# A pairwise embedding product with an MLP on one core: embeddings turned through the U slots and copied by VectorE

## The chip, the cores and the metric

The kernel runs on 1 core of one Trainium2 chip. The metric is the device time of one execution in microseconds (us); lower is better. The kernel before takes 458.64 us, the median of 3 runs (458.62 to 458.97).

The engines are called by the names that the profile uses: PE is TensorE's matmul stream and PEld its weight loads, DVE is VectorE, ACT is ScalarE, POOL is GpSimd and SP is SyncE, which here only issues DMAs.

## The reference

For each of 1024 rows of the batch, 32 embeddings e_0 ... e_31 of 64 numbers are fetched from 32 tables by index. For each of the 496 pairs i < j there is a 64 x 64 matrix K_ij, and the pair's result is one number:

```python
e = stack([tbl_f[ids[:, f]] for f in range(32)], axis=1)      # [1024, 32, 64]
p, q = e[:, ROW_IDX], e[:, COL_IDX]                           # all pairs i < j, 496 of them
z = einsum('bne,hne,bnh->bn', p, kernel, q)                   # z[b, n] = q_n^T K_n p_n
h = concatenate([z, dense_ctx], axis=1)                       # [1024, 496 + 16]
h = maximum(h @ W_top1 + b_top1, 0)                           # 512
h = maximum(h @ W_top2 + b_top2, 0)                           # 256
y = h @ W_top3                                                # [1024, 1]
```

Everything is float32.

## The kernel before

**Tiles and blocks.** The batch is cut into 8 tiles of 128 rows. In a tile the pairs are worked through in 32 blocks (n = 0 to 31). A block has 16 places of 64 numbers: for a pair of fields 2m and 2m+1 (the two halves) it holds the products with up to 8 lower fields i. `plan_blocks` (L44) lays the blocks out in four groups of 2, 6, 10 and 14 blocks; group g needs fields up to 8g+7.

**One block.** PE computes U = K times the turned embedding of the upper field into a U slot, two PSUM banks of `u_ps`. There are three slots (`USLOTS`, L70), used in turn, so PE can be at most three fills ahead of DVE. `block_u` (L374) waits for the slot with `multiplied`, and for the turned embedding with `side_copied`. DVE (`multiply`, L314) multiplies the slot by the lower embedding into SBUF, which frees the slot. Blocks come in two kinds of 16 each. In a straight block the batch row is on the partitions, and the sums over 64 numbers are made by ACT (12 places at most, one activation with an accumulator read each, L264) and DVE (4 places, one reduce, L346), in the order of the blocks; products wait for ACT in a ring of 5 buffers. Straight blocks have one matmul per half ("whole", 8 of them) or two ("split", 8 of them, two DVE products). In a turned block the batch row is on the free axis, 16 matmul records fill the slot, and the sums are made by PE: `pick_sums` (L400) multiplies the product by a 0/1 matrix, 8 matmuls per block (16 records), into the bank `side_ps`.

**The side bank.** `side_ps` is one PSUM bank that all other PE work goes through, step by step: `bank_steps` (L142) writes the order of its uses down, and PE may start a step only when ACT has copied the one before (`side_free`, L360). Its uses in a tile are the four `turn_group` steps, which turn the next tile's embeddings (128x128 transposes against the identity, four per group, L370) and which ACT copies to `emb_t` (L255); the picks of the first eight turned blocks and of the last eight, each in two runs of four; and, for the tile before, `spread` (h0 turned, L421), `hidden1` (L425), `hidden2` (L430) and `logit` (L434). All engines work through their own list in order. The list of PE places these steps after fixed blocks (L136 to L139): 

```python
LATE_SUMS_AT = (0, 2)
MLP_AT = {5: "spread", 8: "hidden1", 11: "hidden2", 13: "logit"}
SUMS_AT = (20, 22)
TURN_AT = {24: 0, 26: 1, 28: 2, 30: 3}
```

In tile 0 each group is turned just before its first block. ACT copies a turned group in its own order, between its sums.

**Loads.** POOL gathers the embeddings with one indirect DMA per field, 32 per tile, in order of tile and field (L222), into three buffers; a fourth tile's gathers wait until the first is used up. PE waits for a group's eight gathers before it turns it. SP issues the indices of all tiles (128 KB), the identity, then all 16 K loads of 512 KB at once, with the pick matrix after the fourth; then the dense features, the weights and the biases. PE's first wait is for the identity and the pick matrix together.

## Time and profile before

| | |
|---|---|
| median of 3 runs | 458.64 us |
| the profiled execution's own time | 458.04 us |
| its span, first to last instruction | 456.2 us |
| mean granted TensorE clock | 0.985 |
| PE busy | 398.2 us (87%), 5424 matmul records |
| PEld busy | 303.2 us (66%) |
| DVE busy | 342.2 us (75%), 448 instructions |
| ACT busy | 337.5 us (74%), 2937 instructions |
| POOL busy | 241.9 us (53%) |

Busy time is the time in which the engine executes at least one instruction; matmuls are pipelined, so a busy PE isn't PE at its peak. A second look at the same execution is the map of its 40 slices of 11.4 us each (a digit is the busy share of the slice in tenths; for PEclk it is the granted clock in tenths; for DMA the busy share of the queues). It shows three stretches: a start of four or five slices with the DMA queues full and PE mostly idle, a long regular stretch, and a short end.

```
PE   0354959899989999899989999999989998999986
DVE  0036857797988798787888798778888798779880
ACT  1048554798778996798778986798769986898662
POOL 5777777777777777777777776377700000000000
PEclk9998879999999999999999999999999999999999
DMA  8991111111111111111111111011100000000000
```

The profiler lists, for the whole span, which engine sat idle and what ended each wait. A wait is a loss only where the waiting engine is the one that others wait for.

### The profile page before, as it was taken

Reading aid. Unit: us, or ns where it says so; the run is one execution under the profiler, and the core shown is the slowest. Engines: PE = TensorE matmul, PEld = TensorE weight load, DVE = VectorE, ACT = ScalarE, POOL = GpSimd, SP = SyncE. Lnnn points to the kernel's source line nnn. Section 1 sums busy time; section 2 is a strip of 40 time slices with the busy share of each in tenths; the row PEclk is TensorE's granted clock in tenths of the full one; section 3 lists DMA queues with packets and bytes.
Section 4 is the critical chain, followed back from the end, with each engine's and each line's share of the span. In section 5 each row is a group of like instructions: output and inputs, shape, how many; then the busy total and the mean of one; then the engine's idle time right before and its main releaser. Section 6 shows DMA issues by size and latency. Waiting matters only on the chain.

```text
span 456.2 us, 15136 instructions
## 1 busy us (share of the span) xinstructions
PE 398.2 (87%) x5424; PEld 303.2 (66%) x5424; DVE 342.2 (75%) x448; ACT 337.5 (74%) x2937; POOL 241.9 (53%) x260
## 2 busy tenths in 40 slices
PE   0354959899989999899989999999989998999986
PEld 0232647677767767677767867777767776777765
DVE  0036857797988798787888798778888798779880
ACT  1048554798778996798778986798769986898662
POOL 5777777777777777777777776377700000000000
PEclk9998879999999999999999999999999999999999
DMA  8991111111111111111111111011100000000000
GB/s 273 385 309 30 27 27 27 30 28 28 30 28 29 29 28 27 29 31 27 30 28 29 28 28 27 12 29 26 29 7 4 2 3 1 4 1 1 4 3 0
DMA packets 14553, 19.62 MB, mean 43 GB/s; under 512 B 7176, under 2 KB 7824, under 8 KB 14480
## 3 DMA queue, kind: packets, MB, share of 16 engines
q0 software_dynamic: 8192, 8.40, 9.9%
q1 hardware_dynamic: 6288, 10.27, 6.6%
q8 instruction: 43, 0.70, 0.7%
q14 instruction: 30, 0.25, 0.2%
HBM read 18.65 MB, written 0.00 MB: 41 GB/s over the span
## 4 chain that ended last, share of the span: by engine, by line
PE 52%; DVE 18%; ACT 13%; issue 11%; POOL 3%; DMA 2%; DVEq 0%
PE u_ps L387 15%; PE side_ps L409 12%; PE u_ps L394 12%; DVE prod_s L336 11%; ACT prod_s L264 10%; PE side_ps L425 7%; DVE h L346 4%; PE side_ps L430 3%; POOL emb L222 3%; DVE prod_t L323 3%; PE side_ps L370 2%; DMA emb<-tbl,ids_sb 1%; ACT emb_t L255 1%; DMA ids_sb<-ids 1%; ACT h_t L278 1%
## 5 line engine op out<-in xcount | busy, mean ns | idle before, releaser
L264 ACT ACTIVATE prod_s<-prod_s 128x64 f32<-128x64 f32 x1408 | 297.0, 324 | 62.4 <-DVE prod_s L336 61.6
L222 POOL DMA_INDIRECT emb<-tbl,ids_sb x256 | 241.7, 944 | 89.2 <-issue 77.4
L264 ACT ACTIVATION_READ_ACCUMULATOR prod_s<-prod_s 128x1 f32 x1408 | 276.0, 239 | 0.0
L336 DVE TENSOR_TENSOR prod_s<-u_ps,emb 128x384 f32<-128x384 f32 (+3 forms) x192 | 159.2, 860 | 53.3 <-PE u_ps L394 53.3
L323 DVE TENSOR_TENSOR prod_t<-u_ps,emb_t 128x1024 f32<-128x1024 f32 x128 | 155.9, 1218 | 46.9 <-PE u_ps L387 46.8
L387 PEld LDWEIGHTS u_ps<-emb_t,k_sb 64*128 64x128 f32 x2048 | 130.5, 192 | 54.2 <-issue 40.2
L387 PE MATMUL u_ps<-emb_t,k_sb 64*128 64x128 f32 x2048 | 144.7, 284 | 16.2 <-ACT emb_t L255 10.8
L394 PE MATMUL u_ps<-k_sb,emb_t 64*128 64x512 f32 (+4 forms) x768 | 141.8, 485 | 1.4 <-ACT emb_t L255 1.4
L394 PEld LDWEIGHTS u_ps<-k_sb,emb_t 64*128 64x128 f32 x768 | 61.5, 195 | 19.2 <-issue 14.6
L409 PEld LDWEIGHTS side_ps<-prod_t,pick_sb 128*32 128x32 f32 x2048 | 54.1, 110 | 13.9 <-issue 13.1
L409 PE MATMUL side_ps<-prod_t,pick_sb 128*32 128x128 f32 x2048 | 62.5, 274 | 0.0
L346 DVE TENSOR_REDUCE h<-prod_s 128x4 f32<-128x256 f32 x128 | 52.4, 410 | 0.3
L370 PE MATMUL side_ps<-id_sb,emb 128*128 128x128 f32 x128 | 21.7, 294 | 31.1 <-DMA emb<-tbl,ids_sb 23.0
L370 PEld LDWEIGHTS side_ps<-id_sb,emb 128*128 128x128 f32 x128 | 14.0, 146 | 41.9 <-issue 33.0
L255 ACT ACTIVATE emb_t<-side_ps 128x512 f32<-128x512 f32 x32 | 21.8, 682 | 25.3 <-PE side_ps L370 25.3
L425 PE MATMUL side_ps<-h_t,w_sb 128*128 128x128 f32 x256 | 30.7, 278 | 4.1 <-ACT h_t L278 4.1
L425 PEld LDWEIGHTS side_ps<-h_t,w_sb 128*128 128x128 f32 x256 | 29.2, 192 | 5.7 <-ACT h_t L278 5.7
L273 ACT ACTIVATE h_t<-side_ps 128x128 f32<-128x128 f32 x16 | 6.2, 389 | 19.9 <-PE side_ps L409 19.9
L430 PEld LDWEIGHTS side_ps<-h_t,w_sb 128*128 128x128 f32 x128 | 14.9, 191 | 6.7 <-issue 5.3
L430 PE MATMUL side_ps<-h_t,w_sb 128*128 128x128 f32 x128 | 16.4, 281 | 1.2 <-ACT h_t L281 1.2
L281 ACT ACTIVATE h_t<-side_ps,b_sb 128x128 f32<-128x128 f32 x32 | 11.0, 612 | 3.9 <-PE side_ps L425 3.9
L284 ACT ACTIVATE h_t<-side_ps,b_sb 128x128 f32<-128x128 f32 x16 | 5.0, 364 | 3.8 <-PE side_ps L430 3.8
(12 smaller groups left out, 23.6 us busy)
## 6 DMA issues: line engine op xcount, KB each, us to landing
k_sb<-k_pairs SPq DMA_DIRECT2D x16, 512.0 KB, 11.1
emb<-tbl,ids_sb POOLq DMA_INDIRECT x256, 2.4
w_sb<-w SPq DMA_DIRECT2D x1, 1024.0 KB
w_sb<-w SPq DMA_DIRECT2D x1, 512.0 KB
ids_sb<-ids SPq DMA_DIRECT2D x1, 128.0 KB, 2.6
h<-dense SPq DMA_DIRECT2D x8, 8.0 KB
out<-y_row SPq DMA_DIRECT2D x8, 0.5 KB
id_sb<-ident SPq DMA_DIRECT2D x1, 64.0 KB, 2.8
```

The source lines that it names most:

```text
L222: nc.gpsimd.indirect_dma_start(emb[t % EMBS][:, f * EMBED:(f + 1) * EMBED], None, tables[f], bass.IndirectOffsetOnAxis(ap=ids_sb[:, t, f:f ...
L255: nc.scalar.activation(emb_t[t % 2][:, g * GROUP_PAIRS:(g + 1) * GROUP_PAIRS], side_ps[:], ACT.Copy,).then_inc(side_copied, 1)
L264: last = nc.scalar.activation(slot, slot, ACT.Copy, accum_out=acc_ps[:, t % 2, column:column + 1])
L323: last = nc.vector.tensor_tensor(prod_t[at % TRING][:].rearrange("p (h x) -> p h x", h=HALVES), u, low.unsqueeze(1).to_broadcast([P, HALVE ...
L336: last = nc.vector.tensor_tensor(product[:, :, cols], u[:, :, cols], low.unsqueeze(1).to_broadcast([P, HALVES, w * EMBED]), ALU.mult)
L346: nc.vector.tensor_reduce(h0[t][:, column:column + ON_DVE], product[:, cols].rearrange("p (n e) -> p n e", e=EMBED), AX_X, ALU.add,).then_ ...
L370: last = nc.tensor.transpose(side_ps[:, d], emb[t % EMBS][:, 2 * m * EMBED:(2 * m + 2) * EMBED], id_sb[:])
L387: last = nc.tensor.matmul(u[:, half * BANK + d * P:half * BANK + (d + 1) * P], k_sb[rows, n * BANK + d * P:n * BANK + (d + 1) * P], emb_t[ ...
L394: last = nc.tensor.matmul(u[:, half * BANK + s * EMBED:half * BANK + (s + w) * EMBED], emb_t[t % 2][rows, m], k_sb[rows, n * BANK + s * EM ...
L409: last = nc.tensor.matmul(side_ps[quad:quad + QUAD, 0], pick_sb[:, 30 - 2 * place:62 - 2 * place], prod_t[at % TRING][:, d * P:(d + 1) * P ...
L425: last = nc.tensor.matmul(side_ps[:, m], w1_sb[:, c, m * P:(m + 1) * P], h0_t[:, c], start=(c == 0), stop=(c == 3))
L430: last = nc.tensor.matmul(side_ps[:, m], w2_sb[:, c, m * P:(m + 1) * P], h1_t[:, c], start=(c == 0), stop=(c == 3))
```

## The change

1. **Turning.** The embeddings are no longer turned through `side_ps` by 128x128 transposes and copied by ACT. Each pair of fields is turned by two transposes of 64 batch rows each, one into each bank of a U slot, and DVE copies the slot to `emb_t`. A turn is thus a use of the U slots like a block's; `slot_uses` writes the order down, and `slot_filled` and `slot_emptied` count fills and copies or products. From tile 1 on, a tile is turned in two parts of eight pairs (16 fields), after blocks 24 and 28 of the tile before. In tile 0 there are seven parts: four pairs, then six times two.
2. **Block order.** The kinds and the order of the blocks in groups 1 to 3 are changed so that blocks come in order of the parts they need. There are again 16 turned and 16 straight blocks (8 whole, 8 split); the places that ACT sums are the same in number. The ring of turned products has 11 buffers in place of 10.
3. **Picks.** The picks of eight turned blocks come in one run: the first eight after block 21, preceded by the logit of the tile before, which lies in the same bank beside them; the last eight after block 6 of the next tile, followed by the transposes of h0 into other columns of the same bank, and ACT copies both at once. hidden1 comes after block 10, hidden2 after block 14.
4. **Loads.** The indices of tile 0 (16 KB) are loaded first, the others after the identity. K loads 1 to 15 wait on SP for the gathers of a part of tile 0; the pick matrix comes after the last K load, with a semaphore of its own. In `w1_rows` the rows of W_top1 are put in the new order on the host.

The core of the diff:

```diff
-    order = ["SS", "STSTSS", "TSTSTSTSTS", "TSTTSTTSTTSTTS"]
+    order = ["SS", "TSSTSS", "TSTTSTSTSS", "TSTTSTSTTSTTTS"]
...
-        turned = [fulls.pop(0) for _ in range(order[a].count("T"))]
-        straight = [x, *fulls, y]
-        blocks += [(turned.pop(0), True) if kind == "T" else (straight.pop(0), False) for kind in order[a]]
+        blocks += zip([*fulls[:2 * a], x, *fulls[2 * a:], y], [kind == "T" for kind in order[a]], strict=True)
...
+FIRST_PARTS = [(0, 4), (4, 6), (6, 8), (8, 10), (10, 12), (12, 14), (14, 16)]
+PARTS = [(0, 8), (8, 16)]
+PART_OF = [next(p for p, (_, stop) in enumerate(FIRST_PARTS) if max(m for m, _, _, _ in b) < stop) for b in BLOCKS]
+FIRST = [PART_OF.index(p) for p in range(len(FIRST_PARTS))]
...
-TRING = 10
+TRING = 11
...
+K_WITH_PART = [4, 6, 8, 10, 12, 14, 16]
+TURN_AT = {24: 0, 28: 1}
...
+def slot_uses():
...
             if t == 0 and n in FIRST:
...
+                uses.append(("turn", 0, FIRST.index(n)))
+            uses.append(("u", t, n))
+            if t + 1 < TILES and n in TURN_AT:
+                uses.append(("turn", t + 1, TURN_AT[n]))
...
+SPREAD_AT, HIDDEN1_AT, HIDDEN2_AT, SUMS_AT = 6, 10, 14, 21
...
-            pool.wait_ge(ids_loaded, 16)
+            pool.wait_ge(first_ids_loaded, 16)
             for t in range(TILES):
+                if t == 1:
+                    pool.wait_ge(ids_loaded, 16)
...
-            sp.dma_start(ids_sb[:], ids.rearrange("(t p) f -> p t f", p=P)).then_inc(ids_loaded, 16)
+            by_tile = ids.rearrange("(t p) f -> p t f", p=P)
+            sp.dma_start(ids_sb[:, 0], by_tile[:, 0]).then_inc(first_ids_loaded, 16)
             sp.dma_start(id_sb[:], ident).then_inc(id_loaded, 16)
-            for c in range(NB // K_PER_LOAD):
-                cols = slice(c * K_PER_LOAD * BANK, (c + 1) * K_PER_LOAD * BANK)
-                sp.dma_start(k_sb[:, cols], k_pairs[:, cols]).then_inc(k_loaded[c], 16)
-                if c == 3:
-                    sp.dma_start(pick_sb[:], pick).then_inc(id_loaded, 16)
+            sp.dma_start(ids_sb[:, 1:], by_tile[:, 1:]).then_inc(ids_loaded, 16)
+            c = 0
+            for p, stop in enumerate(K_WITH_PART):
+                while c < stop:
+                    if c == 1 or (c > 1 and c == K_WITH_PART[p - 1]):
+                        first, last = FIRST_PARTS[p]
+                        sp.wait_ge(first_gathered[p], 16 * 2 * (last - first))
+                    cols = slice(c * K_PER_LOAD * BANK, (c + 1) * K_PER_LOAD * BANK)
+                    sp.dma_start(k_sb[:, cols], k_pairs[:, cols]).then_inc(k_loaded[c], 16)
+                    c += 1
+            sp.dma_start(pick_sb[:], pick).then_inc(pick_loaded, 16)
...
-            def copy_turned(t, g):
-                act.wait_ge(side_ready, READY[f"turn{g}", t])
-                if t >= 2:
-                    act.wait_ge(multiplied, (t - 1) * NB)
-                nc.scalar.activation(emb_t[t % 2][:, g * GROUP_PAIRS:(g + 1) * GROUP_PAIRS], side_ps[:], ACT.Copy,
-                                     ).then_inc(side_copied, 1)
...
+            def copy_first_sums(t):
+                act.wait_ge(picked, t * NT + CHUNK)
+                if t > 0:
+                    copy_logit(t - 1)
+                nc.scalar.activation(h0_t[:, 0], side_ps[:, 0], ACT.Copy).then_inc(side_copied, 1)
+            def copy_spread(t):
+                act.wait_ge(mlp_mm, 3 * t + 1)
+                nc.scalar.activation(h0_t[:, 1:], side_ps[:, :3], ACT.Copy).then_inc(side_copied, 1)
...
                     if not TURNED[n]:
                         sum_block(t, n)
+                    if t > 0 and n == 0:
+                        copy_acc(t - 1)
+                    if t > 0 and n == SPREAD_AT:
+                        copy_spread(t - 1)
+                    if t > 0 and n == HIDDEN1_AT:
+                        hidden1(t - 1)
+                    if t > 0 and n == HIDDEN2_AT:
+                        hidden2(t - 1)
+                    if n == SUMS_AT:
+                        copy_first_sums(t)
...
+            def copy_turned(t, part):
+                at = SLOT_USE["turn", t, part]
+                dve.wait_ge(slot_filled, at + 1)
+                first, last = FIRST_PARTS[part] if t == 0 else PARTS[part]
+                turned_half = u_ps[at % USLOTS][:].rearrange("p (h m b) -> p m h b", h=HALVES, b=P // 2)
+                nc.vector.tensor_copy(emb_t[t % 2][:, first:last, :].rearrange("p m (h b) -> p m h b", h=HALVES),
+                                      turned_half[:, :last - first]).then_inc(slot_emptied, 1)
...
                     multiply(t, n)
+                    if t + 1 < TILES and n in TURN_AT:
+                        copy_turned(t + 1, TURN_AT[n])
                     if n > 0 and not TURNED[n - 1]:
                         sum_block(t, n - 1)
...
-            def turn_group(t, g):
-                pe.wait_ge(gathered[t % EMBS][g], 16 * GROUP * (t // EMBS + 1))
-                side_free(f"turn{g}", t)
...
+            def slot_free(at):
+                if at >= USLOTS:
+                    pe.wait_ge(slot_emptied, at - USLOTS + 1)
+                return u_ps[at % USLOTS]
+            def turn_part(t, part):
+                if t == 0:
+                    first, last = FIRST_PARTS[part]
+                    pe.wait_ge(first_gathered[part], 16 * 2 * (last - first))
+                else:
+                    first, last = PARTS[part]
+                    fills = t // EMBS if t % EMBS == 0 else t // EMBS + 1
+                    pe.wait_ge(gathered[t % EMBS][part], 16 * 2 * (last - first) * fills)
+                u = slot_free(SLOT_USE["turn", t, part])
+                for m in range(first, last):
+                    for half in range(HALVES):
+                        rows = slice(half * P // 2, (half + 1) * P // 2)
+                        at = half * BANK + (m - first) * P // 2
+                        done = nc.tensor.transpose(u[:, at:at + P // 2],
+                                                   emb[t % EMBS][rows, 2 * m * EMBED:(2 * m + 2) * EMBED],
+                                                   id_sb[rows, rows])
+                done.then_inc(slot_filled, 1)
...
+            def spread(t):
+                pe.wait_ge(side_copied, STEPS * t + 1)
+                pick_sums(t, 1)
+                pe.wait_ge(summed_v, (t + 1) * NS)
+                pe.wait_ge(acc_copied, t + 1)
+                for c in range(S_CHUNKS):
+                    last = nc.tensor.transpose(side_ps[:, 1 + c], h0[t][:, c * P:(c + 1) * P], id_sb[:])
+                last.then_inc(mlp_mm, 1)
...
                 for n in range(NB):
                     if t == 0 and n in FIRST:
-                        turn_group(0, FIRST.index(n))
+                        turn_part(0, FIRST.index(n))
                     block_u(t, n)
...
+                    if t > 0 and n == SPREAD_AT:
+                        spread(t - 1)
+                    if t > 0 and n == HIDDEN1_AT:
+                        hidden1(t - 1)
+                    if t > 0 and n == HIDDEN2_AT:
+                        hidden2(t - 1)
+                    if n == SUMS_AT:
+                        if t > 0:
+                            logit(t - 1)
+                        else:
+                            pe.wait_ge(pick_loaded, 16)
+                        pick_sums(t, 0)
                     if t + 1 < TILES and n in TURN_AT:
-                        turn_group(t + 1, TURN_AT[n])
+                        turn_part(t + 1, TURN_AT[n])
```

## Rows read from the trace of the kernel before

**Rows 1.** Windows, one regular tile: length, PE, PEld, DVE, ACT, POOL, clock, DMA, GB/s

```profile
218.56:269.33 50.77, 48.49 (x680) 36.99 (x681) 42.74 (x57) 41.89 (x370) 38.58 (x41) 1.00 0.16 29
```

**Rows 2.** Waits in that tile: who for whom, us in total, times, longest

```profile
DVE prod_t L323 <- PE u_ps L387: 4.7, 5, 1.5
DVE prod_s L336 <- PE u_ps L394: 3.3, 2, 2.3
...
PE side_ps L370 <- ACT emb_t L255: 1.2, 1, 1.2
...
PE side_ps L425 <- ACT h_t L278: 0.5, 1, 0.5
```

**Rows 3.** PE in order of time, tile 0: start us, duration us, what

```profile
44.91 2.08 PE L387 MATMUL u_ps<-emb_t,k_sb 64*128 64x128 f32 x16 [5.88 <-ACT emb_t L255]
...
63.13 2.08 PE L387 MATMUL u_ps<-emb_t,k_sb 64*128 64x128 f32 x16 [4.94 <-ACT emb_t L255]
...
85.24 0.66 PE L370 MATMUL side_ps<-id_sb,emb 128*128 128x128 f32 x4
```

**Rows 4.** POOL in order of time, the 1st, 48th and 64th gather

```profile
3.61 1.08 POOL L222 DMA_INDIRECT emb<-tbl,ids_sb  x1 [3.17 <-DMA ids_sb<-ids]
...
62.43 0.94 POOL L222 DMA_INDIRECT emb<-tbl,ids_sb  x1 [0.30 <-issue]
...
82.40 0.94 POOL L222 DMA_INDIRECT emb<-tbl,ids_sb  x1 [0.30 <-issue]
```

**Rows 5.** Gathers between 60 and 90 us, from issue to landing

```profile
DMA to landing us min/median/max: 2.2/2.4/3.3
```

**Rows 6.** DVE in order of time; first and last are block 31

```profile
87.11 1.29 DVE L336 TENSOR_TENSOR prod_s<-u_ps,emb 128x128 f32<-128x128 f32 x2
...
231.65 1.21 DVE L323 TENSOR_TENSOR prod_t<-u_ps,emb_t 128x1024 f32<-128x1024 f32 x1
232.78 0.41 DVE L346 TENSOR_REDUCE h<-prod_s 128x4 f32<-128x256 f32 x1
...
243.35 1.29 DVE L336 TENSOR_TENSOR prod_s<-u_ps,emb 128x128 f32<-128x128 f32 x2 [0.98 <-PE u_ps L394]
244.55 0.41 DVE L346 TENSOR_REDUCE h<-prod_s 128x4 f32<-128x256 f32 x1
244.88 1.28 DVE L336 TENSOR_TENSOR prod_s<-u_ps,emb 128x384 f32<-128x384 f32 x2
...
441.05 1.28 DVE L336 TENSOR_TENSOR prod_s<-u_ps,emb 128x128 f32<-128x128 f32 x2
```

**Rows 7.** PE in order of time, the regular stretch

```profile
226.71 2.06 PE L387 MATMUL u_ps<-emb_t,k_sb 64*128 64x128 f32 x32
228.70 0.66 PE L370 MATMUL side_ps<-id_sb,emb 128*128 128x128 f32 x4
229.28 1.13 PE L394 MATMUL u_ps<-k_sb,emb_t 64*128 64x512 f32 x4
...
240.17 1.96 PE L409 MATMUL side_ps<-prod_t,pick_sb 128*32 128x128 f32 x64
242.05 2.11 PE L394 MATMUL u_ps<-k_sb,emb_t 64*128 64x64 f32 x16
...
252.83 3.84 PE L425 MATMUL side_ps<-h_t,w_sb 128*128 128x128 f32 x32 [0.52 <-ACT h_t L278]
...
259.41 2.05 PE L430 MATMUL side_ps<-h_t,w_sb 128*128 128x128 f32 x16
```

**Rows 8.** PE at the end of the last tile

```profile
439.87 3.70 PE L409 MATMUL side_ps<-prod_t,pick_sb 128*32 128x128 f32 x128
```

**Rows 9.** ACT in the chain that ended last, a whole block's sums

```profile
249.90 2.57 ACT prod_s L264 x24
```

**Rows 10.** The chain that ended last, its first DMA: start us, us

```profile
0.74 2.60 DMA ids_sb<-ids
```

**Rows 11.** Windows, the 2 us after tile 0's second wait for ACT (clock third last)

```profile
64.00:66.00 2.00, 2.00 (x18) 1.98 (x18) 0.74 (x1) 0.00 (x0) 1.56 (x2) 0.50 0.24 41
```

More of the change, by code:

```diff
@@ L113, in w1_rows @@
 def w1_rows():
[L114 to L118 removed]
+    rows = [None] * (T_CHUNKS * P)
     for n in range(NB):
@@ L124, in w1_rows @@
                     chunk, quad, place = sum_place((T_INDEX[n] * HALVES + half) * LOW + d // 2)
[L125 to L144 removed]
+                    rows[chunk * P + quad + 2 * place + d % 2] = pair_row(i0 + d, 2 * m + half)
+    straight = [n for n in range(NB) if not TURNED[n]]
+    rows += [pair_row(i, j) for n in straight for s, i, j in places(n) if s in act_slots(n)]
+    rows += [pair_row(i, j) for n in straight for s, i, j in places(n) if s not in act_slots(n)]
+    return rows + list(range(PAIRS, PAIRS + DENSE))
+K_PER_LOAD = 2
+K_WITH_PART = [4, 6, 8, 10, 12, 14, 16]
+TURN_AT = {24: 0, 28: 1}
+def slot_uses():
+    uses = []
     for t in range(TILES):
@@ L438, in _, with hidden1 @@
-            pe.wait_ge(id_loaded, 32)
+            def spread(t):
[6 more added lines that the diff above has]
+                last.then_inc(mlp_mm, 1)
+            def hidden1(t):
+                pe.wait_ge(side_copied, STEPS * t + 2)
+                for m in range(4):
+                    for c in range(4):
+                        last = nc.tensor.matmul(side_ps[:, m], w1_sb[:, c, m * P:(m + 1) * P], h0_t[:, c],
+                                                start=(c == 0), stop=(c == 3))
+                last.then_inc(mlp_mm, 1)
@@ new lines, in hidden2, with logit @@
+            def hidden2(t):
+                pe.wait_ge(side_copied, STEPS * t + 3)
+                for m in range(2):
+                    for c in range(4):
+                        last = nc.tensor.matmul(side_ps[:, m], w2_sb[:, c, m * P:(m + 1) * P], h1_t[:, c],
+                                                start=(c == 0), stop=(c == 3))
+                last.then_inc(mlp_mm, 1)
+            def logit(t):
+                pe.wait_ge(side_copied, STEPS * t + 4)
+                for c in range(2):
+                    last = nc.tensor.matmul(side_ps[0:1, 1], w3_sb[:, c:c + 1], h2_t[:, c],
+                                            start=(c == 0), stop=(c == 1))
+                last.then_inc(logit_mm, 1)
@@ L439, in _ @@
+            pe.wait_ge(id_loaded, 16)
             for t in range(TILES):
```

184 lines of the change are left out of this document (61 added, 123 removed).

## The prediction

> **What bounds the kernel now.** I read the map of slices first, for the stretches; then the windows and the waits of one tile of the regular stretch; then DVE and PE in order of time; and then the start, PE's waits beside POOL's clock of gathers.
>
> A regular tile takes 50.77 us, with PE busy 48.49, DVE 42.74 and ACT 41.89 [rows 1]. DVE waits 8.0 us per tile for PE (4.7 + 3.3); PE's waits for ACT are only 1.2 (a turned group's copy) and 0.5 (the copy of h0) [rows 2]. So PE sets the pace, and DVE runs dry while PE does side work, since only three slots lie between them.
>
> In tile 0 PE waits 5.88 and 4.94 us for ACT, whose copies of turned groups queue behind its sums; its last turn of tile 1's embeddings starts at 85.24 [rows 3]. That is close behind the 64th gather, issued at 82.40 [rows 4], which with the median landing of 2.4 us [rows 5] is there at 84.8. POOL needs 1.25 us per gather, 40 per tile: tile 0 to tile 1 is bound by POOL within half a microsecond, whatever PE and ACT do before.
>
> I lay the time out by one mark, the start of DVE's product of block 31. It is at 87.11 in tile 0 and 441.05 in tile 7 [rows 6], so the span of 456.2 is 87.1 (start), 6 x 50.77 = 304.6, 49.3 for tile 7, and 15.15 (end).
>
> **Prices.** DVE, from one start to the next: a turned product 1.13, a reduce 0.33, a split product 1.20, followed by its own reduce 1.33 (87.11 to 88.44 also is one, as block 31) [rows 6]. A whole product moves as many numbers as a turned one; I take 1.13 too. PE: a turned block 0.99, a split block 1.02, a whole one 0.86 to 0.97, four transposes with their switches of mode 0.58, 64 pick records 1.88, hidden1 3.8, hidden2 2.0 [rows 7]. 128 pick records in one run take 3.70 to the modelled end [rows 8], against 1.96 for 64, so a run of eight blocks is 1.88 + 1.74 = 3.62 and saves 0.14 against two of four. A result is seen by DVE 0.13 after PE has passed on. A slot is free for PE 0.14 after the product's end (duration 1.21, or 1.28 split).
>
> **The DVE copies** (added, not in the trace). Each moves 1024 numbers per partition out of PSUM. The nearest row is the turned product, 1024 from PSUM at 1.13. From below half of that row, 0.57, since the product reads two operands and a copy one. From above 1.3, if the strided destination costs. I take 1.13. Two per tile: DVE's work goes from 42.0 to 44.3.
>
> The Trainium skill, "VectorE: DVE Perf Modes", section "Why PSUM operands drop a tier", says that an operand in PSUM holds float32 work to one number per cycle. By it the lower bound falls away and the copy is 1.07 plus overhead; no row here shows a plain copy on DVE, only the product, which agrees (1.13).
>
> **The 64-row transposes** (16 per part). From below 0.03 us each, as a pick record (1.88 / 64); from above 0.06, as a record of a turned block (0.99 / 16): 0.5 to 1.0 per part, I take 0.8. Before, two groups took 1.16. Up to 1.0 it is hidden: behind block 24 DVE is 2 us behind PE. PE also drops the 1.2 of wait and eight changes of mode per tile.
>
> **The regular tile afterwards,** walked from the start of DVE's product of block 31 (time 0). In each segment DVE works off what it has, PE does its side work, and DVE's idle is the difference.
>
> Blocks 31, 0 to 6. DVE: 1.66 + 1.20 + 1.52 + 1.46 + 1.13 + 1.52 + 1.46 + 1.13 = 11.1 (products with the reduces behind them). PE is slot-bound: it may start block 6 when block 3's slot is free, at 5.8 + 1.35 = 7.2, and has passed it at 8.15. Then the run of eight picks and the transposes of h0, 3.62 + 0.3: to 12.05; block 7 is ready at 13.2. DVE idles 2.1.
> Blocks 7 to 10. DVE works to 18.8. PE: three blocks to 15.9, hidden1 to 19.7, block 11 at 20.8. Idle 2.0.
> Blocks 11 to 14. DVE to 25.7; PE to 23.6, hidden2 to 25.6, block 15 at 26.7. Idle 1.0.
> Blocks 15 to 21. DVE 9.3 of work, to 36.0. PE is slot-bound again: block 21 is passed at 33.2; logit and eight picks 4.0, to 37.2; block 22 at 38.3. Idle 2.3.
> Blocks 22 to 30 and two copies. DVE 13.5, without a gap, to 51.8. PE waits for slots.
>
> So a tile is 44.3 of DVE work and 7.4 of idle, 51.8 us: 1.0 more than now. DVE's idle falls only from 8.0 [rows 2] to 7.4: PE's waits for ACT are gone (1.7), but eight picks at once outlast three full slots by more than two runs of four did, and give 1.1 back; the copies add 2.3 of work. PE's own savings turn into waits for slots. ACT is no longer in the way: a whole block's sums take 2.4 us [rows 9], a split one's 2.0; in the walk they are through block 6 at 14.2, h0 is copied at 14.9, and PE asks at 15.9. What is late next is DVE in blocks 22 to 31. If this cover of 1 us on ACT is gone, each us is a us per tile. Ring waits: the product of block 7 needs the sums of block 0, done at 5.3 against 13.2. The eleventh turned buffer covers block 10's need of the ninth turned block, picked in the run after block 6.
>
> **The start.** The first indices are 16 KB; with 128 KB the DMA took 2.60 [rows 10]. From below nothing, from above 0.6 (the fixed part is most of it); I take 0.3: the 64th gather lands at 84.5. The K loads now wait for gathers, so SP's queue (K, pick, dense, weights) is stretched to about 45 + 15 us: the last K is issued when tile 0's gathers are in, at 45, and weights are asked for at about 90. It is all covered by what follows. The finer parts and DVE's copies let PE finish block 24 of tile 0 near 50, where now it sits behind ACT. But PE then stands at the turn after block 24, which wants 16 fields of tile 1, the 48th gather: 62.4 + 2.4 - 0.3 = 64.5. Blocks 25 to 28 follow. Then the turn after block 28 wants all 32: 84.5. Blocks 29 to 31 of tile 0 and the whole of tile 1 are queued behind it. Now they aren't: the last turn comes after block 30. So the mark, block 31's product, comes at 84.5 + turn 0.8 + 2 x 0.99 + 1.15 = 88.4 at full clock. But PE has then idled some 13 us, and after 4.94 of idle the granted clock was 0.50 [rows 11], the lower of the two levels, 1.2 GHz; a turned block took 2.08 in place of 1.16 [rows 3]. With turn and both turned blocks at half clock it is 84.5 + 1.5 + 2.1 + 1.8 + 1.3 = 91.2. I take 90.7, which is 3.6 later than 87.1 (1.3 to 4.1). The gains in tile 0, 10.8 us of ACT waits, go into the wait for POOL.
>
> **Tile 7 and the end.** No copies after blocks 24 and 28: 51.8 - 2.3 = 49.5 (now 49.3). The end keeps its chain; the copy of the second picks falls away, 0.3: 14.85.
>
> **Sum.** 90.7 + 6 x 51.8 + 49.5 + 14.85 = 465.9 of span, against 456.2: 9.7 more, or 467.7 against the profiled execution's own 458.04. The median lies 0.6 above that execution. I predict 468.2.
>
> **Rivals.**
> A, the copies run at half price (0.57): DVE's work is 43.2, a tile 50.7. The start still loses 3.6: 468.2 - 6 x 1.1 = 461.6. For it speaks that a copy has one source; against it every row from PSUM. 7 in 100.
> B, PE keeps the pace, the other side: PE loses two transposes' modes, two pick switches and its waits, 30.9 for blocks, 3.9 + 3.8 + 2.0 + 4.0 side work, 1.6 turns, 0.4 switches = 46.6. If DVE's idle shrank to what is left, PE's present 2.3 of waits would give a tile of 48.9: 7 x 1.9 = 13.3 less, 3.6 more at the start: 449. It decides where DVE's idle falls below 5.9 (a tile of 50.2), since 7 x 0.52 = 3.6 pays for the start. Against it: three slots hold 3.4 us of products and each run of eight is 3.9. 8 in 100.
> The Trainium skill, "TensorEngine Tiling (Array Packing)", section "Key Properties", says that changing the tiling mode drains TensorE. The rows agree in kind: four transposes with their changes take 0.58. By that rule PE gains, as in B; it doesn't help where DVE sets the end.
> C, a smaller loss: the walk is 0.9 too long per tile (runs of eight cheaper, whole products overlapped), and PE's clock comes back quickly: 50.9 per tile, mark at 89: 461. 20 in 100.
> D, a larger one: ACT's copies queue behind sums at hidden1, or copies at 1.3: 52.5 per tile: 473. 12 in 100.
> E, nothing measurable: a tile of 50.2 pays exactly for the start: 458.6. 5 in 100.
> The forecast itself, 465 to 471, has 48 in 100.
>
> **Range and chances.** 460 to 473.5 takes in A, C and the forecast, and most of D. Faster by over 0.2% 0.10 (B, and 2 of C's 20 should its pieces go further), within 0.2% (what a measurement of this kernel can't tell from no change) 0.05 (E), slower 0.85 (the rest).
>
> **What would show it.** PE should sit idle until about 64.5 and again until about 84.5, both times waiting for the gathers of tile 1, with the clock low behind. Block 31's product of tile 0 should start near 90.7 and that of the next tiles every 51.8 us. DVE busy per tile should be about 45, PE's about 46.5, ACT's 39. PE's waits should name DVE (slots) in blocks 15 to 31; DVE's idle should be near 7.4 in four pieces of 1 to 2.3, behind blocks 6, 10, 14 and 21. The copies should show 1.2 each. I am wrong if tile 1 starts before 86, or if a tile takes under 50.8.

## The result, and the profile after

The kernel after takes 469.9 us (median of 4 runs, 469.52 to 470.17), the kernel before 458.63 beside it (4 runs, 458.55 to 458.97). The ratio is 1.024, its 95% interval 1.0226 to 1.0254: slower by 11.3 us. The forecast was 468.2, in a range of 460 to 473.5.

The profiled execution took 470.17, with a span of 468.4. By the same mark as in the prediction (the start of block 31's product on DVE) that is 89.81 (start) + 6 x 52.00 + 49.74 (tile 7) + 16.84 (end). Before it was 87.11 + 6 x 50.77 + 49.3 + 15.15. So of the 12.2 us in the span 2.7 came in the start, 7.4 in six regular tiles, 0.4 in tile 7 and 1.7 at the end.

First a regular tile of the kernel after, in the view of windows (length; busy time of PE, PEld, DVE, ACT and POOL; clock; DMA share; GB/s), which answers to [rows 1]:

```profile
193.83:245.84 52.01, 48.75 (x696) 37.33 (x694) 44.67 (x60) 39.60 (x362) 36.80 (x39) 1.00 0.14 28
```

Then its waits, which answer to [rows 2]:

```profile
DVE prod_s L370 <- PE u_ps L440: 4.8, 2, 2.4
...
DVE prod_t L357 <- PE u_ps L433: 2.5, 2, 1.8
...
PE u_ps L433 <- DVE prod_t L357: 0.9, 3, 0.3
...
PE u_ps L440 <- DVE prod_s L370: 0.8, 2, 0.5
```

No row names ACT as what PE waited for any more, DVE works 1.9 us longer than before, and DVE's idle time is 7.3 in place of 8.0. The sum of work and idle is what the tile takes: 44.7 + 7.3 = 52.0. PE now has small waits for DVE, that is for slots. DVE in order of time, same tile, shows where the 7.3 lie, and one of the two copies:

```profile
207.36 1.29 DVE L370 TENSOR_TENSOR prod_s<-u_ps,emb 128x128 f32<-128x128 f32 x2 [2.39 <-PE u_ps L440]
...
214.87 1.23 DVE L357 TENSOR_TENSOR prod_t<-u_ps,emb_t 128x1024 f32<-128x1024 f32 x1 [1.84 <-PE u_ps L433]
...
220.56 1.22 DVE L357 TENSOR_TENSOR prod_t<-u_ps,emb_t 128x1024 f32<-128x1024 f32 x1 [0.68 <-PE u_ps L433]
...
232.33 1.23 DVE L370 TENSOR_TENSOR prod_s<-u_ps,emb 128x1024 f32<-128x1024 f32 x1 [2.39 <-PE u_ps L440]
...
236.12 1.22 DVE L344 COPY emb_t<-u_ps 128x1024 f32<-128x1024 f32 x1
237.25 1.22 DVE L357 TENSOR_TENSOR prod_t<-u_ps,emb_t 128x1024 f32<-128x1024 f32 x1
```

The copy starts at 236.12 and the next product at 237.25, so it holds DVE for 1.13. PE around the first gap, and one fill that waited for its slot:

```profile
202.06 3.70 PE L453 MATMUL side_ps<-prod_t,pick_sb 128*32 128x128 f32 x128
205.70 0.44 PE L466 MATMUL side_ps<-id_sb,h 128*128 128x128 f32 x2
206.07 1.25 PE L440 MATMUL u_ps<-k_sb,emb_t 64*128 64x64 f32 x8
207.15 1.06 PE L433 MATMUL u_ps<-emb_t,k_sb 64*128 64x128 f32 x16
...
226.04 1.16 PE L433 MATMUL u_ps<-emb_t,k_sb 64*128 64x128 f32 x16 [0.29 <-DVE prod_t L357]
```

PE is away from the blocks from 202.06 to 206.07, and DVE has worked off its three slots before that.

The start, PE in order of time, answers to [rows 3]:

```profile
66.60 1.14 PE L440 MATMUL u_ps<-k_sb,emb_t 64*128 64x192 f32 x8 [2.10 <-DVE emb_t L344]
67.57 0.66 PE L418 MATMUL u_ps<-id_sb,emb 64*128 64x64 f32 x16
68.06 2.27 PE L433 MATMUL u_ps<-emb_t,k_sb 64*128 64x128 f32 x32
...
83.93 1.12 PE L418 MATMUL u_ps<-id_sb,emb 64*128 64x64 f32 x16 [11.33 <-DMA emb<-tbl,ids_sb]
84.84 3.73 PE L433 MATMUL u_ps<-emb_t,k_sb 64*128 64x128 f32 x32
```

POOL's first and 64th gather ([rows 4]), the load of the first indices ([rows 10]), and the mark ([rows 6]), each from its view in order of time or of DMA issues:

```profile
2.71 1.08 POOL L239 DMA_INDIRECT emb<-tbl,ids_sb  x1 [2.26 <-DMA ids_sb<-ids]
...
81.49 0.94 POOL L239 DMA_INDIRECT emb<-tbl,ids_sb  x1 [0.30 <-issue]
```

```profile
ids_sb<-ids SPq DMA_DIRECT2D x1, 16.0 KB, 1.7
```

```profile
89.81 1.29 DVE L370 TENSOR_TENSOR prod_s<-u_ps,emb 128x128 f32<-128x128 f32 x2
```

Windows of 2 us behind PE's wait (the clock is the third number from the end), as [rows 11]:

```profile
84.00:86.00 2.00, 2.00 (x26) 2.00 (x28) 0.90 (x1) 0.00 (x0) 1.70 (x2) 0.50 0.21 33
86.00:88.00 2.00, 2.00 (x24) 2.00 (x22) 1.73 (x3) 0.00 (x0) 1.39 (x3) 0.50 0.09 16
88.00:90.00 2.00, 2.00 (x20) 1.62 (x20) 1.52 (x3) 0.00 (x0) 1.61 (x2) 0.78 0.17 33
90.00:92.00 2.00, 2.00 (x26) 1.49 (x24) 1.97 (x5) 0.87 (x9) 1.47 (x2) 1.00 0.15 27
```

PE waited 11.33 us for the last gathers of tile 1, 2.44 after the 64th was issued, and then ran for 4 us at the lower clock: the transposes took 1.12, where the same 16 took 0.66 at 67.57. The end, PE in order of time and then windows:

```profile
455.53 0.41 PE L466 MATMUL side_ps<-id_sb,h 128*128 128x128 f32 x2 [1.45 <-ACT h L285]
456.52 5.47 PE L473 MATMUL side_ps<-h_t,w_sb 128*128 128x128 f32 x32 [0.58 <-ACT h_t L296]
```

```profile
456.00:458.00 2.00, 1.48 (x11) 1.48 (x12) 0.00 (x0) 0.47 (x1) 0.00 (x0) 0.88 0.00 0
458.00:460.00 2.00, 2.00 (x11) 2.00 (x11) 0.00 (x0) 0.00 (x0) 0.00 (x0) 0.50 0.00 0
460.00:462.00 2.00, 1.99 (x14) 1.79 (x12) 0.00 (x0) 0.00 (x0) 0.00 (x0) 0.77 0.00 0
```

hidden1 of the last tile took 5.47, against 3.84 at full clock [rows 7], because the clock was down at 0.50.

### The profile page after: what moved, and what is told of

The parts are those of the page before. It is cut to its first block, busy times and chain, and to the rows that moved or that the text cites. A ratio compares the mean times of both kernels' runs of the same rounds, so it can differ in the third digit from the quotient of the medians.

```text
span 468.4 us, 15338 instructions
## 1 busy us (share of the span) xinstructions
PE 400.9 (86%) x5552; PEld 308.8 (66%) x5552; DVE 358.9 (77%) x469; ACT 319.2 (68%) x2897; POOL 241.9 (52%) x260
## 4 chain that ended last, share of the span: by engine, by line
PE 42%; DVE 28%; issue 15%; POOL 13%; ACT 1%; DMA 1%; DVEq 0%
DVE prod_s L370 14%; POOL emb L239 13%; PE side_ps L453 11%; DVE prod_t L357 10%; PE u_ps L433 10%; PE u_ps L440 9%; PE side_ps L473 7%; PE side_ps L481 3%; DVE h L380 3%; PE side_ps L488 1%; PE side_ps L466 1%; DVE emb_t L344 1%; DMA emb<-tbl,ids_sb 1%; ACT prod_s L280 0%; DMA ids_sb<-ids 0%
## 5 line engine op out<-in xcount | busy, mean ns | idle before, releaser
L280 ACT ACTIVATE prod_s<-prod_s 128x64 f32<-128x64 f32 x1408 | 295.5, 380 | 128.6 <-DVE prod_s L370 128.0
L370 DVE TENSOR_TENSOR prod_s<-u_ps,emb 128x640 f32<-128x640 f32 (+4 forms) x192 | 157.9, 860 | 44.5 <-PE u_ps L440 44.5
L433 PEld LDWEIGHTS u_ps<-emb_t,k_sb 64*128 64x128 f32 x2048 | 134.9, 195 | 60.2 <-DVE prod_s L370 20.9
L357 DVE TENSOR_TENSOR prod_t<-u_ps,emb_t 128x1024 f32<-128x1024 f32 x128 | 155.1, 1216 | 24.6 <-PE u_ps L433 24.6
L433 PE MATMUL u_ps<-emb_t,k_sb 64*128 64x128 f32 x2048 | 148.7, 287 | 17.6 <-DVE prod_t L357 6.4
L440 PE MATMUL u_ps<-k_sb,emb_t 64*128 64x512 f32 (+4 forms) x768 | 146.2, 489 | 15.0 <-DVE emb_t L344 6.1
L453 PE MATMUL side_ps<-prod_t,pick_sb 128*32 128x128 f32 x2048 | 60.4, 273 | 0.0
L344 DVE COPY emb_t<-u_ps 128x1024 f32<-128x1024 f32 (+2 forms) x21 | 20.2, 963 | 24.9 <-PE u_ps L418 24.9
L418 PE MATMUL u_ps<-id_sb,emb 64*128 64x64 f32 x256 | 12.9, 237 | 29.1 <-DMA emb<-tbl,ids_sb 27.1
L418 PEld LDWEIGHTS u_ps<-id_sb,emb 64*128 64x128 f32 x256 | 11.5, 148 | 35.6 <-issue 18.1
L481 PEld LDWEIGHTS side_ps<-h_t,w_sb 128*128 128x128 f32 x128 | 14.9, 192 | 6.7 <-issue 5.3
L301 ACT ACTIVATE h_t<-side_ps,b_sb 128x128 f32<-128x128 f32 x32 | 9.7, 451 | 5.6 <-PE side_ps L473 5.6
L296 ACT ACTIVATE h_t<-side_ps 128x384 f32<-128x384 f32 x8 | 7.7, 968 | 0.6 <-PE side_ps L466 0.6
```

The costliest lines, as they stand in the source:

```text
L280: last = nc.scalar.activation(slot, slot, ACT.Copy, accum_out=acc_ps[:, t % 2, column:column + 1])
L344: nc.vector.tensor_copy(emb_t[t % 2][:, first:last, :].rearrange("p m (h b) -> p m h b", h=HALVES), turned_half[:, :last - first]).then_in ...
L357: last = nc.vector.tensor_tensor(prod_t[at % TRING][:].rearrange("p (h x) -> p h x", h=HALVES), u, low.unsqueeze(1).to_broadcast([P, HALVE ...
L370: last = nc.vector.tensor_tensor(product[:, :, cols], u[:, :, cols], low.unsqueeze(1).to_broadcast([P, HALVES, w * EMBED]), ALU.mult)
L418: done = nc.tensor.transpose(u[:, at:at + P // 2], emb[t % EMBS][rows, 2 * m * EMBED:(2 * m + 2) * EMBED], id_sb[rows, rows])
L433: last = nc.tensor.matmul(u[:, half * BANK + d * P:half * BANK + (d + 1) * P], k_sb[rows, n * BANK + d * P:n * BANK + (d + 1) * P], emb_t[ ...
```

## The experiments

All but the fourth, which is the kernel before with the new loads, start from the kernel after. Each time is a median, and each ratio is against the kernel before, run beside it on the same chip. One thing is needed to read them. On the three chips of the first nine runs every kernel took 747 to 777 us, the one before 775.0 to 776.7. As long as POOL was issuing gathers there, PE's matmuls came late: by ones and twos with up to 2.4 us of idle time between them, and in the start with single gaps of up to 63 us. The map of 40 slices of the version with all parts shows it, as do PE and POOL in order of time:

```profile
PE   2001002488218982199722996149951499999997
...
POOL 6777773001760027500374004730057200000000
```

```profile
121.59 0.94 POOL L272 DMA_INDIRECT emb<-tbl,ids_sb  x1 [0.30 <-issue]
184.23 0.94 POOL L272 DMA_INDIRECT emb<-tbl,ids_sb  x1 [61.70 <-DVE prod_s L418]
```

```profile
121.44 2.08 PE L495 MATMUL u_ps<-k_sb,emb_t 64*128 64x192 f32 x8 [62.76 <-issue]
...
184.11 1.16 PE L488 MATMUL u_ps<-emb_t,k_sb 64*128 64x128 f32 x16
185.20 1.37 PE L508 MATMUL side_ps<-prod_t,pick_sb 128*32 128x128 f32 x33
...
191.35 0.43 PE L508 MATMUL side_ps<-prod_t,pick_sb 128*32 128x128 f32 x2 [1.11 <-issue]
192.78 0.44 PE L508 MATMUL side_ps<-prod_t,pick_sb 128*32 128x128 f32 x2 [0.99 <-issue]
```

The low digits of PE (0 to 2) stand over high ones of POOL, and within 3 us of POOL's next gather at 184.23 PE's records come by ones and twos, with idle time that is put down to "issue", no wait. ACT and DVE have such gaps too (57.1 and 19.0 us at the longest in the first 130 us). The cause isn't shown. One more reading fits late loading of instructions: on the instruction queues (q8 and q14 of the DMA view) 2 packets moved in the first 122 us of this run and 7 in POOL's pause up to 184, where the kernel after, in its own measurement, moved 14 in its first 122 us with POOL gathering all the time. But an engine that stands still also asks for fewer.

So the totals and the start can't be read there, not even their sign: the kernel after with one turn moved is faster than the kernel before on these chips (ratio 0.9885). The tiles behind the last gather run at clock 1.00 with POOL at 0.00, and they can: a tile of the fourth kernel, which has the block code of the one before, takes 50.77 there, as in [rows 1]. I use only those. The last three runs were on a fourth chip, without this (before: 458.53).

**One turn later**: the second part after block 30.

```diff
-TURN_AT = {24: 0, 28: 1}
+TURN_AT = {24: 0, 30: 1}
```

> The changed kernel, with the second turn of the next tile after block 30 in place of 28. Theory (in tile 0 PE stands at this turn for the 64th gather, landed at 83.9, and blocks 29 to 31 are queued behind it): with blocks 29 and 30 done before the wait, block 31's product of tile 0 starts near 87 in place of 89.8, tiles stay at 52.0, time 467. Rival (the K loads in step with gathers, or SP's stretched queue, set the start): the mark stays at 89.8, time 469.9.

767.16 against 776.69, ratio 0.9885 (0.987 to 0.9901). A tile behind the gathers:

```profile
648.03:700.03 52.00, 48.62 (x696) 37.34 (x694) 44.66 (x59) 39.61 (x362) 0.00 (x0) 1.00 0.01 2
```

52.00: where the turn stands costs nothing in a tile, and this is the tile of the kernel after to compare the next ones with. What it does to the start can't be read, and it was not run on a chip without the delay.

**Only one pair copied** (from tile 2 on the copies move 1 pair of 8; the rest of `emb_t` keeps old values).

```diff
+                if t > 1:
+                    last = first + 1
```

> The changed kernel; from tile 2 on DVE copies only the first of the eight turned pairs of a part, so emb_t keeps old numbers for the others and the output isn't the reference's. Theory (DVE sets the pace between block 21 and block 6, so each us of copy is a us of the tile): a copy of about 0.2 in place of 1.13, twice per tile, gives tiles of 50.2 in place of 52.0; 12 copies, 11 us, time 459. Rival (PE sets the pace, copies are hidden): tiles 52.0, time 469.9.

754.18, ratio 0.9707 (0.9692 to 0.9721).

```profile
638.83:688.96 50.13, 47.37 (x697) 37.34 (x694) 42.79 (x59) 39.61 (x362) 0.00 (x0) 1.00 0.01 2
```

The tile lost 1.87, DVE's busy time 1.87: what a copy takes from DVE, the tile gets.

**Picks in runs of four** (the first chunk after blocks 17 and 21, the second after 2 and 6).

```diff
+LATE_HALF_AT, SUMS_HALF_AT = 2, 17
...
-                    if n == SUMS_AT:
+                    if n == SUMS_HALF_AT:
...
-                        pick_sums(t, 0)
+                        pick_sums(t, 0, 0)
+                    if n == SUMS_AT:
+                        pick_sums(t, 0, 1)
```

> The changed kernel with the picks in runs of four again: the first eight after blocks 17 (behind the logit) and 21, the last eight after blocks 2 and 6. Theory (a run of eight outlasts three full slots, DVE idles 2.4 behind each): DVE's idle per tile falls from 7.3 to about 6.2, tiles 50.9, time 462. Rival (runs of eight save PE changes of mode and cost nothing): two runs more, tiles 52.0 to 52.3, time 470 to 472.

775.1, ratio 0.9974 (0.9961 to 0.9988). The tile and DVE's waits in it:

```profile
660.02:710.99 50.97, 47.83 (x696) 37.04 (x694) 44.75 (x59) 39.42 (x362) 0.00 (x0) 1.00 0.01 2
```

```profile
DVE prod_t L359 <- PE u_ps L435: 5.2, 3, 2.8
DVE prod_s L372 <- PE u_ps L442: 1.0, 2, 0.6
```

DVE's work is the same (44.75), its idle falls from 7.3 to 6.2, the tile by 1.03. Runs of eight in place of fours cost 1.03 per tile. (The logit went with the first picks, from block 21 to block 17; it wasn't moved alone.)

**The kernel before with the new loads** (first indices alone, K in step with gathers, pick matrix last).

```diff
+                    if c == 1 or (c > 1 and c == K_WITH_PART[p - 1]):
+                        sp.wait_ge(first_gathered[p], 128 if p == 0 else 64)
```

> The kernel before with the new loads alone: the indices of tile 0 first, K loads in step with the gathers of tile 0, the pick matrix last. Theory (POOL's gathers bind the first tile change, the K loads are covered): the 64th gather lands 0.9 earlier, block 31's product of tile 0 at 86.2 to 87.1, time 457.7 to 458.6. Rival (K loads in step starve tile 0 and are what delays the changed kernel's start): the mark comes 2 to 4 later, time 461 to 463.

776.15, ratio 0.999 (0.9981 to 0.9999); a tile 50.77. What the loads do to the start of that kernel wasn't seen, since the start is where PE's instructions were late. It stays open. Two windows of this run show the size of the delay, one in which POOL gathers and one in which it waits:

```profile
190.00:230.00 40.00, 12.74 (x36) 5.28 (x37) 0.05 (x1) 2.97 (x27) 29.19 (x31) 0.56 0.13 27
240.00:280.00 40.00, 38.03 (x495) 29.36 (x494) 33.69 (x42) 31.58 (x275) 0.00 (x0) 1.00 0.01 2
```

**Copies on ACT** from tile 1 on, each as two activations of 512, between its sums.

```diff
+                for half in range(HALVES):
+                    turned_half = u_ps[at % USLOTS][:, half * BANK:half * BANK + (last - first) * P // 2]
+                    done = nc.scalar.activation(
+                        emb_t[t % 2][:, first:last, half * P // 2:(half + 1) * P // 2],
+                        turned_half.rearrange("p (m b) -> p m b", b=P // 2), ACT.Copy)
```

> The changed kernel with ACT in place of DVE copying the turned parts of tiles 1 to 7 out of the U slots (in ACT's order before its sums of blocks 24 and 27). Theory (DVE's work plus its idle make the tile): DVE's work falls by 2.3 us a tile, its idle stays 7.3, ACT's rises to 42: tiles of 49.7, against 52.0; on a chip where the kernel before takes 458.6 the time is 455 to 456. Rival (the turns through the slots, not the copy engine, cost the time, or ACT answers late and holds a slot): tiles of 51 or more, 464 or more.

746.86 against 774.97, ratio 0.964 (0.9624 to 0.9656).

```profile
628.93:678.67 49.74, 47.14 (x698) 37.47 (x696) 42.39 (x58) 41.46 (x366) 0.00 (x0) 1.00 0.01 2
```

49.74, the 2.26 of two copies less, with DVE's waits unchanged (4.8 + 2.5). ACT has the room.

**PE kept busy at the end** with 6 and 2 unused matmuls in the waits of the last tile.

```diff
+                if t == TILES - 1:
+                    warm(6)
```

> The changed kernel with six unused matmuls on PE where it waits for the last sums of tile 7 and two more ahead of hidden1, so that it doesn't idle there. Theory (hidden1 of the last tile took 5.47 in place of 3.84 because the granted clock fell behind the two waits of PE): it takes 3.84 again, the end 15.2 in place of 16.8, time 468.3. Rival (the fall of the clock has nothing to do with these waits): 5.5 as before, plus up to 0.5 for the unused matmuls, time 470.

765.59, ratio 0.9882 (0.9861 to 0.9903). hidden1 took 3.84 and the end 15.2. But the later turn, without such matmuls, had 3.84 and 15.13 on those chips too. So it shows nothing of the cause. The fourth run speaks against the change as the cause. Its PE code is that of the kernel before, with waits at the end like those of before (1.52 and 0.47), and its hidden1 was slow:

```profile
763.84 5.47 PE L445 MATMUL side_ps<-h_t,w_sb 128*128 128x128 f32 x32 [0.47 <-ACT h_t L290]
```

**Tile 1 turned late**: in four parts, after blocks 24 and 28 of tile 0 and after 3 and 12 of tile 1.

```diff
+SECOND_AT = {(0, 24): 0, (0, 28): 1, (1, 3): 2, (1, 12): 3}
+SECOND_PARTS = [(0, 4), (4, 8), (8, 12), (12, 16)]
```

> The changed kernel with tile 1's embeddings turned in four parts of four pairs, after blocks 24 and 28 of tile 0 and after blocks 3 and 12 of tile 1 itself, so that tile 1 may start before its last gathers. Theory (the wait for the 64th gather with blocks 29 to 31 behind it is what the start costs): no wait of PE for a gather above 2 us after 64, block 31's product of tile 0 starts at 75 to 79 in place of 89.8, tiles after the first at 52.0, time 456 to 460 where the kernel before takes 458.6. Rival (tile 0 is bound by ACT's sums or K loads whatever the gathers do): the mark at 86 or later, time above 466.

764.16, ratio 0.9867 (0.9848 to 0.9887); a tile 52.00. The start again can't be read.

**All together**: ACT copies, runs of four, tile 1 late, PE kept busy at the end; and the same kernel once more on another chip.

> All together: tile 1 turned late, picks in runs of four, turned parts of tiles 2 to 7 copied by ACT, unused matmuls in PE's waits at the end. Theory, adding the pieces: mark of tile 0 near 77, tiles of 52.0 - 2.3 - 1.0 = 48.7, end 15.2: 77 + 6 x 48.7 + 48.5 + 15.2 = 433 of span, 435 in time where the kernel before takes 458.6. Rival (PE, with 48.7 us of busy time a tile, becomes the bound before that): tiles of 49.5 to 50.5, 440 to 446.

> The kernel of the last run again (all four pieces). In the runs so far PE's instructions came one by one, up to 2.4 us apart, while POOL issued gathers, in the kernel before too (775 against 458.6 in the first measurement), so totals and starts can't be read from them; tiles that ran after the last gather can. Without that delay, by the theory: no wait for the 64th gather with blocks 29 to 31 behind it, block 31's product of tile 0 at 75 to 79 (89.8 in the changed kernel), tiles of 48.7, time 435 where the kernel before takes 458.6. Rival (tile 0 is bound by ACT's sums or by K loads, not by tile 1's gathers): the mark at 86 or later, 445 or more. With the delay: about 756 against 775 again, and nothing learnt of the start.

756.35 against 774.97, ratio 0.9756 (0.974 to 0.9773); again 759.96 against 776.73, ratio 0.9768 (0.9745 to 0.9792). A tile, in the first of them:

```profile
641.86:690.57 48.71, 46.23 (x698) 37.15 (x696) 42.49 (x57) 41.31 (x366) 0.00 (x0) 1.00 0.01 2
```

48.71 both times: 52.00 - 2.26 - 1.03 = 48.71, the two parts add up without loss. The second run met the same delay and taught nothing of the start.

**Fields by plain loads from SP**, three runs. POOL issues nothing; SP loads 128 consecutive rows of each table in place of the gathered ones. Paced: with small loads in between, so that the 64 fields of the first two tiles take until 95.5; fast: without them (`False` for `True`); and the version with all parts, paced.

```diff
-                    nc.gpsimd.indirect_dma_start(
+                sp.dma_start(emb[t % EMBS][:, f * EMBED:(f + 1) * EMBED], tables[f][row:row + P, :]).then_inc(arrived, 16)
+                    gaps = 2 if True and t < 3 else 0
```

> The changed kernel with the gathers left out: SP loads fixed rows of the same tables, one plain DMA of the same size per field, and two small unused DMAs (or a K, pick, dense or weight load) behind each in tiles 0 to 2, so that 64 fields arrive at about POOL's pace. POOL does nothing. The output isn't the reference's. Two questions. First, is it POOL's gathers that hold PE's instructions back on these chips? If so, PE runs as in the first measurement and tiles are 52.0 from the start; if not, totals stay above 700. Second, the start. Theory (the 64th field's arrival decides, with turn, blocks 29 to 31 behind it): PE waits for it, and block 31's product of tile 0 starts 5 to 7 us after PE's turn, at 90 to 98 with three issues of about 0.45 us per field. Rival (K loads, ACT's sums or tile 0's own work set it): no wait of PE over 3 us at that turn.

> As the last, without the small unused DMAs: the fields come one every 0.5 us and all 64 are there by 45 to 50 us. Theory: no wait for tile 1's fields; block 31's product of tile 0 starts at 58 to 70, set by tile 0's own work, tiles stay at 52.0 (DVE's work and idle don't know of the loads), time 437 to 450. Rival (something else in the start costs the time): the mark stays within 5 us of the paced kernel's.

> The kernel with all four pieces (tile 1 turned late, picks in runs of four, ACT's copies, unused matmuls at the end), with the loads of the paced kernel. The output isn't the reference's. Theory: the same arrivals as in the paced kernel, but block 31's product of tile 0 starts 12 to 20 us earlier than there, since tile 1's last 32 fields no longer stand in its way; tiles 48.7; time 28 to 42 less than the paced kernel's. Rival: PE meets the same wait a few blocks later and tile 1 gives it all back, so that block 31's product of tile 1 is no earlier than 48.7 behind the paced kernel's mark.

Paced: 481.86 against 458.53, ratio 1.0506 (1.0463 to 1.0549). Fast: 453.79, ratio 0.9908 (0.9872 to 0.9945). All parts, paced: 462.44, ratio 1.009 (1.006 to 1.0121). PE at the second turn of tile 1's fields, paced; the same turn, fast; and the mark, fast (DVE):

```profile
95.53 1.12 PE L436 MATMUL u_ps<-id_sb,emb 64*128 64x64 f32 x16 [17.51 <-DMA emb<-tbl]
```

```profile
69.20 0.72 PE L436 MATMUL u_ps<-id_sb,emb 64*128 64x64 f32 x16 [0.30 <-DVE prod_t L375]
```

```profile
74.95 1.28 DVE L388 TENSOR_TENSOR prod_s<-u_ps,emb 128x128 f32<-128x128 f32 x2
```

The code is the same but for when fields arrive, the tiles are the same (51.99), and the mark moves from 100.96 to 74.95, so 26.0 of the 28.1 between the two medians lie in the start, the rest at the end (16.98 and 15.18). The arrival of tile 1's last field sets the mark, in the paced run 5.4 after the turn and in the kernel after 5.88 after it. I had expected the fast run's mark at 58 to 70 and its time at 437 to 450, and missed both (453.79): tile 0's own work takes until 75, so the wait for gathers costs the kernel after at most 89.81 - 74.95 = 14.9 us.

In the version with all parts PE waits inside tile 1 instead:

```profile
125.17 1.12 PE L489 MATMUL u_ps<-id_sb,emb 64*128 64x64 f32 x16 [4.52 <-DMA emb<-tbl]
...
147.52 1.12 PE L489 MATMUL u_ps<-id_sb,emb 64*128 64x64 f32 x16 [15.36 <-DMA emb<-tbl]
```

Its mark of tile 0 is 79.88, 21 us earlier than the paced 100.96, and its mark of tile 1 is 153.04, against 152.95. The rival was right: all of the 21 us is given back, because the fields of tile 2 come no earlier. The time is 19.4 less than the paced run's, not 28 to 42. What it gains (18.9 of span) is five tiles at 3.3, tile 7 and the end.

This doesn't carry over to the gathers as it stands. These paced loads brought tile 2's 32 fields in 52.0 us (95.53 to 147.52), longer than a tile of 48.7; POOL's gathers take 40 us for 32. In the trace of the kernel after the 96th gather is issued at 121.43. Landed 2.44 later, as the 64th was, and with the 5.52 from turn to mark of this run, it would let tile 1's mark start at 129.4, against 141.82 in the kernel after (tile 0's mark at 79.88 and a tile of 48.7 would allow 128.6). So with gathers most of what the late turn gains should stay. This is an estimate; no run shows it.

Whether it is POOL's gathers that delay PE on the other chips could not be told, since on this chip the kernel before wasn't delayed at all.

## Why the prediction was right

The sign, the mechanism and the time came as forecast. By its steps:

- **What sets the pace of a tile.** Forecast: DVE's work plus its idle behind PE's side work, 44.3 + 7.4 = 51.8. Measured 44.7 + 7.3 = 52.00 (rivals C and D stood at 50.9 and 52.5). The profile counts a product before a gap to its end, 1.22, the forecast only 1.13, to where the next could start. In the forecast's own measure the tile is 44.3 of work and 7.65 of idle, so the work was right and the idle 0.25 short. The four gaps were to be 2.1, 2.0, 1.0 and 2.3; in that measure they are 2.5, 1.9, 0.8 and 2.5 (2.39, 1.84, 0.68 and 2.39 in the view). Part of it is a misread price: a result was to be seen by DVE 0.13 after PE has passed on, and block 7, passed at 207.15, is seen at 207.36, 0.21 after. ACT's sums of a whole block were taken as 2.4, where [rows 9] has 2.57; the cover held, since hidden1 starts without a wait. Shown piece by piece: shorter copies (-1.87), no copies on DVE (-2.26) and shorter runs (-1.03) each moved the tile by that much. Against before, the copies add 2.26 and the runs of eight 1.03; what is left of the change, ACT out of PE's way and the new order, gives 2.06 back (50.77 - 48.71). This is by subtraction; its parts weren't taken apart.
- **The copy**, taken at 1.13 between 0.57 and 1.3: 1.13, and 1216 ns long on average:

```profile
L344 DVE COPY emb_t<-u_ps 128x1024 f32<-128x1024 f32 x14 | 17.0, 1216 | 10.0 <-PE u_ps L418 10.0
```

  That settles rival A. The Trainium skill, "VectorE: DVE Perf Modes", section "Why PSUM operands drop a tier", says that a PSUM operand takes float32 work down to one number per cycle; this copy agrees, at the duration of a product with two operands.
- **The runs of eight**, 1.1 per tile: 1.03 in the run with fours. **Transposes**, taken at 0.8 (0.5 to 1.0): 0.49 from 67.57 to 68.06, at the lower end, hidden as it was meant to be.
- **PE's busy time**, forecast 46.5, was 48.75. This is mostly the measure: the price of 0.99 is from one fill's start to the next, but the record of a fill lasts 1.16, to its modelled end. Where PE waits behind a fill, up to 0.17 of the wait counts as busy, and some 14 such waits a tile would make the difference (an estimate). With fewer waits it comes down (46.23 with all parts). It cost nothing, since DVE sets the pace.
- **Rival B** (PE keeps the pace, 48.9 per tile) needed DVE's idle below 5.9. Runs of four take it to 6.2, and a tile of 48.7 was seen only without the copies.
- **The start.** Forecast 90.7, measured 89.81. The wait, the queue behind the turn after block 28, and the lower clock behind the wait came as forecast. The term of the first indices was too small: POOL began 0.9 earlier (2.71 against 3.61), not 0.3, since the 16 KB load took 1.7, 0.9 less than the 2.60 of [rows 10]. That is 0.6 of the 0.9; the other 0.3 lies between turn and mark, 5.88 against the 6.2 that I took, where the forecast had chosen between 3.9 at full clock and 6.7 at half.
- **The step that failed** is "PE should sit idle until about 64.5", at the turn after block 24. Block 24 was to be done near 50 and was started at 66.60, so that turn, at 67.57, found its fields there. The 50 doesn't follow from the prediction's own numbers: in the kernel before PE reached this turn at 76.39, and without the 10.8 us of waits for ACT that would be 65.6. What the runs showed in their place: up to that turn the kernel before waits 12.2 us for ACT's copies, and the kernel after 12.2 us for DVE's, since behind each small part PE stands until it is copied (0.5 to 0.8 for the first three, 2.1 to 2.9 for the last four, as at 66.60). PE is there 8.8 us earlier, mostly because it waits less for gathers (15.8 against 23.0). None of it moves the mark, which the 64th gather sets either way. So this step was wrong without cost, because the next one, which was right, covers it. The fast plain loads show where tile 0's work alone would end: 75.
- **The end**, forecast 14.85, measured 16.84, is the largest miss. The copy that was to fall away (0.3) gave nothing: with the clock up the end is 15.18 (fast plain loads), against 15.15 before. The other 1.66 is hidden1 at the lower clock. The paced plain loads had it too (5.46), and so had the kernel before with the new loads (5.47); the other seven traces without unused matmuls had 3.84. The waits ahead of it are nearly those of before (1.45 and 0.58, against 1.53 and 0.47). What brings the clock down in one execution and not in another stays open, and these 1.66 can't be called a cost of the change. Without them the profiled execution would be some 10.5 us slower than the one before, the forecast's own 9.7 and 0.8 more.

The misses, -0.9 + 6 x 0.2 + 0.2 + 2.0, are 2.5 of span; the median lies 0.3 below the profiled execution, where the forecast had it 0.5 above its own, which takes 0.8 back: 1.7 is left.

**What remains open:** on a chip where gathers don't delay PE, the K loads alone on the kernel before, the turn after block 30, tile 1 turned late, and the version with all parts. For the last an estimate from the measured parts, with the mark where it is in the kernel after, is 89.8 + 6 x 48.7 + 48.7 + 15.2 = 446 of span, some 448 us; with tile 1's mark at 129.4, as worked out above, it is 129.4 + 5 x 48.7 + 48.7 + 15.4 = 437. Either would beat both kernels; it was run only where the kernel before takes 775 (ratio 0.976).

## What to carry to other kernels

Taking a copy from the engine that seems in the way and giving it to the one whose products set the pace costs its full length: walk the pacing engine through one period, work and idle apart, before moving anything onto it. Side work of PE should come in pieces no longer than what the slots between PE and the next engine hold; here runs of four in place of eight were worth 1.03 us per tile, though a run of eight is shorter in itself (3.64 against twice 1.88). And look what sets the start before speeding it up: here it was the arrival of the next tile's fields. A faster turn can't move that; turning those fields later can, as far as the loads run ahead of the tiles.

## What the runs showed of the hardware

- The kernel before took 458.5 us on the chip of the last three runs and 776.7, 775.0 and 776.7 on three others. In the traces from those three PE's matmuls came by ones and twos, with up to 2.4 us of idle time between them and single gaps of up to 63 us, while POOL issued gathers, and without delay while it paused. The excess of the kernel before, 316 to 318 us, is close to 256 gathers at 1.25 us (320), but that of the kernel after with unused matmuls at its end, which has the same 256 gathers, is only 296 (765.59 against 469.9).
- A wait of 11.33 us left PE at the lower clock for 4 us (0.50 until 88, 1.00 from 90). At the end waits of 1.2 to 1.5 and 0.5 to 0.6 us were followed by a hidden1 of 5.46 or 5.47, with the clock down to 0.50 where it was read, in three traces, and by one of 3.84 in seven. The same PE code (that of the kernel before) did either, on two chips.
- 16 transposes of 64 x 64 in float32 take 0.49 us on PE at full clock, from their start to the next fill's, four of 128 x 128 with their changes of mode 0.58.
